# Softmax denominators in two halves, v tiles in halves, and other orders of small work in a graph network kernel

## What is computed

```python
for i in range(NUM_BLOCKS):                       # 4
    y = cond_layer_norm(x, cond, s1_w[i], s1_b[i], b1_w[i], b1_b[i])
    q, k, v = y @ wq[i] + bq[i], y @ wk[i] + bk[i], y @ wv[i] + bv[i]     # 4 heads of 128
    scores = (q[src] * k[dst]).sum(-1) * 128 ** -0.5
    ex = exp(scores - segment_max(scores, src)[src])
    out = segment_sum(ex[..., None] * v[dst], src) / segment_sum(ex, src)
    x = x + out @ wo[i] + bo[i]
    y = cond_layer_norm(x, cond, s2_w[i], s2_b[i], b2_w[i], b2_b[i])
    x = x + relu(y @ m_w1[i] + m_b1[i]) @ m_w2[i] + m_b2[i]
```

## Time and profile before

| quantity | value |
|---|---|
| median of 3 executions | 3040.24 us |
| the profiled execution | 3037.72 us, span of its instructions 3036.0 us |
| PE busy | 2839.1 us |
| DVE busy | 2028.1 us |
| ACT busy | 917.6 us |
| POOL busy | 615.7 us |
| mean granted PE clock | 0.973 of full speed |

### The profile page before, as it was taken

The page is one execution under the profiler, slowest core; times in us unless marked ns, Lnnn a source line. Parts: engine busy times, 40 slices in busy tenths (PEclk is TensorE's granted clock), DMA queues, the critical chain, the costliest instruction groups (busy, mean ns, idle before and its releaser), DMA issues.

```text
span 3036.0 us, 31287 instructions
## 1 busy us (share of the span) xinstructions
PE 2839.1 (94%) x11232; PEld 1806.2 (59%) x11232; DVE 2028.1 (67%) x3758; ACT 917.6 (30%) x1315; POOL 615.7 (20%) x494
## 2 busy tenths in 40 slices
PE   2889989998999999999999999999899999999999
PEld 0346656675556676556666555667545566456555
DVE  8889867786746777757776765778787876623211
ACT  4558732223312223212222221222322213213221
POOL 0000043342113334023334031334310000000000
PEclk9899999999999999999999999999999999999999
DMA  4000020002300000400000320000245244420001
GB/s 108 1 1 1 21 77 1 28 1 66 104 21 1 1 28 15 132 32 14 1 28 15 93 70 14 1 28 1 83 118 152 70 134 137 132 78 37 14 1 34
DMA packets 74966, 143.63 MB, mean 47 GB/s; under 512 B 11684, under 2 KB 12107, under 8 KB 74812
## 3 DMA queue, kind: packets, MB, share of 16 engines
q1 hardware_dynamic: 69276, 129.61, 14.3%
q0 software_dynamic: 5536, 12.03, 1.2%
HBM read 130.68 MB, written 10.92 MB: 47 GB/s over the span
## 4 chain that ended last, share of the span: by engine, by line
PE 73%; DVE 17%; issue 5%; ACT 3%; DMA 1%; DVEq 1%; POOL 0%; POOLq 0%; ACTq 0%
PE ps L1680 14%; PE ps L1903 11%; PE ps L1932 10%; PE ps L1774 6%; PE ps L1877 5%; PE ps L1585 5%; PE ps L1652 4%; DVE prob L1087 4%; DVE x L1077 3%; PE ps L1602 2%; PE ps L1924 2%; PE ps L1763 2%; DVE ps L1030 2%; PE ps L1748 2%; ACT prob L1454 2%
## 5 line engine op out<-in xcount | busy, mean ns | idle before, releaser
L721 POOL TENSOR_TENSOR pacc<-pacc,prob 125x628 f32<-125x628 f32 (+1 forms) x288 | 404.8, 1405 | 349.8 <-DVE prob L1106 349.8
L1680 PE MATMUL ps<-yT,w 128*128 128x416 f32 (+1 forms) x1152 | 439.8, 539 | 15.0 <-DVE qk_lo L1021 5.9
L1774 PE MATMUL ps<-prob,big 125*128 125x314 f32 x1280 | 393.7, 430 | 14.1 <-DVE prob L1106 10.8
L1454 ACT ACTIVATE prob<-prob 125x628 f32<-125x628 f32 x320 | 233.0, 728 | 575.1 <-DVE prob L1087 575.1
L1932 PE MATMUL ps<-pieces,counts_r 125*125 125x512 f32 x1400 | 354.5, 407 | 0.0
L1680 PEld LDWEIGHTS ps<-yT,w 128*128 128x128 f32 x1152 | 227.8, 200 | 201.3 <-issue 187.6
L1106 DVE SCALAR_TENSOR_TENSOR prob<-prob,typed 125x628 f32<-125x628 f32 x320 | 260.2, 813 | 70.2 <-ACT prob L1454 67.6
L1932 PEld LDWEIGHTS ps<-pieces,counts_r 125*125 125x125 f32 x1400 | 258.2, 186 | 77.2 <-issue 17.4
L1763 PE MATMUL ps<-qk_hi 128*125 128x314 f32 x640 | 271.4, 424 | 11.5 <-DVE prob L1087 11.3
L1774 PEld LDWEIGHTS ps<-prob,big 125*128 125x128 f32 x1280 | 227.5, 189 | 81.1 <-DVE prob L1106 27.2
L1030 DVE CUSTOM_DVE_ANT_0 ps<-ps,typed 125x628 f32<-125x628 f32 x320 | 257.8, 816 | 8.0 <-PE ps L1748 7.5
(11 more groups left out here) (222 smaller groups left out, 4282.6 us busy)
## 6 DMA issues: line engine op xcount, KB each, us to landing
basis<-in_basis SPq DMA_DIRECT2D x160, 256.0 KB, 2.7
lite_ring<-in_basis SPq DMA_DIRECT2D x120, 256.0 KB, 2.6
w<-in_m_w SPq DMA_DIRECT2D x8, 1024.0 KB, 6.8
w<-in_wk SPq DMA_DIRECT2D x5, 1024.0 KB, 6.3
w<-in_wv SPq DMA_DIRECT2D x4, 1024.0 KB, 5.6
oT<-in_cw SPq DMA_DIRECT2D x8, 512.0 KB, 3.9
w<-in_wq SPq DMA_DIRECT2D x4, 1024.0 KB, 5.6
w<-in_wo SPq DMA_DIRECT2D x4, 1024.0 KB, 5.5
```

The source lines that it names most:

```text
L721: nc.gpsimd.tensor_tensor(pacc[:, c0:c0 + nn], pacc[:, c0:c0 + nn], prob[:, n % 3, p0:p0 + nn], ALU.add).then_inc(psum_done, 1)
L1454: A.activation(prob[:, n % 3, :], prob[:, n % 3, :], ACT.Exp, scale=DH ** -0.5).then_inc(exp_done, 1)
L1680: last = mm(lin_ps(job, 128, nn), weight[:, k, m * 128:(m + 1) * 128], lhs[:, k, c0:c0 + nn], start=(k == 0), stop=(k == KD - 1))
L1774: last = mm(o_halves[:, b, :], vrow[:, t, h * DH:(h + 1) * DH], prob[:, n % 3, b * QUARTER:(b + 1) * QUARTER], start=(t == 0), stop=(t == ...
```

## The change

1. `row_product` takes the pieces it shall do. In the edge loop a v tile's first two pieces are multiplied at the norm step, the other two four edge steps later.
2. The count copies go to seven places (`TURNED`): three in `prob`, two in `pacc`, two in `shift`. ACT's first `max_row` waits for all masks and for the DMAs out of `shift`, POOL's first sum for those out of `pacc`.
3. In block 0 the second matrices are copied by ACT before the first projection and their low rows made by DVE after its low parts. In later blocks POOL waits for the last `xn` of the norm before it stacks, too.
4. `norm_tiles` does what stands beside the last tile after its last `tile_scale`.
5. The maxima are not negated; the identity by which `max_row` multiplies is.
6. Denominators are made in two halves: tiles 0 to 4 at step 13 (DVE reads them at step 14), tiles 5 to 9 between the second and the third projection of head h+2. Before, all stood behind `max_row`.

Renamed semaphores and tiles are left out of the diff:

```diff
+TURNED = 7
+DEN_AT, DEN_TILES = T + 3, (range(0, T // 2), range(T // 2, T))
+PARTS = {None: range(6), 0: range(0, 1), 1: range(1, 4), 2: range(4, 6), 3: range(2, 6), 4: range(1, 2), 5: range(2, 4)}
...
+        early = w.take()
         project(h + 2, 0)
-        project(h + 2, 1)
+        project(h + 2, 4)
+        g["den"][h] = (early, w.take())
+        project(h + 2, 5)
         max_row(h + 1)
-        g["den"][h] = w.take()
         project(h + 2, 2)
...
+            b = s % TURNED
+            if b < 3:
+                return prob[:].rearrange("p s n -> p (s n)").bitcast(F16)[:, b * N:(b + 1) * N]
+            home = pacc if b < 5 else shift
+            return home[:].bitcast(F16)[:, ((b - 3) % 2) * N:((b - 3) % 2 + 1) * N]
...
-                    if half == 0:
-                        if i == 0:
-                            pool.wait_ge(mneg_ready, 1)
+                    if half == 0 and i:
+                        pool.wait_ge(xn_ready, at(i, 2 * T, T))
                         stack_matrices(1, at(i, 32, 32))
                         nc.gpsimd.drain().then_inc(cw_ready, 1)
...
+                            if i == 0 and n == 0:
+                                for b in (3, 4):
+                                    pool.wait_ge(crow_out[b], 16 * len(range(b, T, TURNED)))
...
-            def matrices_low(signal, count):
-                dve.wait_ge(signal, count)
+            def matrices_low(ln, count):
+                dve.wait_ge(cw_hi, count)
+                mine = cw[:, 2 * ln:2 * ln + 2, :]
                 for rows in (slice(32, 64), slice(96, 128)):
-                    V.tensor_tensor(cw[rows, 0:2, :], stage[rows], cw[rows, 0:2, :].bitcast(F32), ALU.subtract)
+                    V.tensor_tensor(mine[rows], stage[rows], mine[rows].bitcast(F32), ALU.subtract)
...
-                    if t < T and beside is not None:
+                    if t < T - 1 and beside is not None:
                         beside(t)
+                if beside is not None:
+                    beside(T - 1)
...
-                def negate_max(h):
+                def join_max(h):
                     V.drain()
-                    V.tensor_tensor(mx[:], mxp[:, :, 0], mxp[:, :, 1], ALU.max)
-                    V.drain()
-                    V.tensor_scalar(nmx[:], mx[:], -1.0, None, ALU.mult)
-                    V.drain().then_inc(neg_max_ready, 1)
+                    V.tensor_tensor(mxr[:], mxp[:, :, 0], mxp[:, :, 1], ALU.max)
+                    V.drain().then_inc(max_ready, 1)
...
+                if i == 0:
+                    matrices_low(1, 2)
...
+                def reciprocals(h, half):
+                    job, t0, t1 = g["den"][h][half], DEN_TILES[half][0], DEN_TILES[half][-1] + 1
+                    dve.wait_ge(lin_full, job.full)
+                    V.tensor_scalar(rden[:, t0:t1], lin_ps(job, P, t1 - t0, t0), 1.0e-30, None, ALU.max).then_inc(lin_empty[job.slot], 1)
+                    V.drain()
+                    V.reciprocal(rden[:, t0:t1], rden[:, t0:t1])
+                    return V.drain()
...
+                        if j == DEN_AT + 1:
+                            reciprocals(h, 0)
                     if h + 1 < HEADS:
-                        negate_max(h + 1)
+                        join_max(h + 1)
                     if h + 2 < HEADS:
                         low_parts(h + 2, 0)
-                        low_parts(h + 2, 1)
-
-                    job = g["den"][h]
-                    dve.wait_ge(lin_full, job.full)
-                    V.tensor_scalar(rden[:], lin_ps(job, P, T), 1.0e-30, None, ALU.max).then_inc(lin_empty[job.slot], 1)
-                    V.drain()
-                    V.reciprocal(rden[:], rden[:])
-                    V.drain().then_inc(sums_read, 1)
+                        low_parts(h + 2, 4)
+                    reciprocals(h, 1).then_inc(sums_read, 1)
                     if h + 2 < HEADS:
+                        low_parts(h + 2, 5)
                         low_parts(h + 2, 2)
...
-                    matrices_low(cw_hi, i + 2)
+                    matrices_low(0, i + 3)
...
-                if s >= 3:
-                    act.wait_ge(crow_out[s % 3], 16 * (s // 3))
-                    act.wait_ge(mneg_ready, s - 2)
+                if s >= TURNED:
+                    act.wait_ge(crow_out[s % TURNED], 16 * (s // TURNED))
+                    act.wait_ge(mneg_ready, s - TURNED + 1)
...
+                    act.wait_ge(stage_in, 32)
+                    A.activation(cw[:, 2:4, :], stage, ACT.Copy).then_inc(cw_hi, 1)
...
-            def row_product(job, lhs, t, weight):
-
-                reuse(job)
-                for k in range(KD):
+            def row_product(job, lhs, t, weight, parts=range(KD)):
+
+                if 0 in parts:
+                    reuse(job)
+                for k in parts:
                     last = mm(lin_ps(job, P, D), lhs[:, k, t * P:(t + 1) * P], weight[:, k, :],
                               start=(k == 0), stop=(k == KD - 1))
-                last.then_inc(lin_full, 1)
+                if KD - 1 in parts:
+                    last.then_inc(lin_full, 1)
...
-                    row_product(first["v"][t], yT, t, w[0])
+                    row_product(first["v"][t], yT, t, w[0], range(0, 2))
...
+                if rest == NORM_EVERY // 2 and 4 <= n < T + 4:
+                    row_product(first["v"][n - 4], yT, n - 4, w[0], range(2, KD))
...
+                def denominators(h, half):
+                    job = g["den"][h][half]
+                    reuse(job)
+                    pe.wait_ge(psum_done, at(i, EXPS, h * 2 * T + (half + 1) * T))
+                    for t in DEN_TILES[half]:
+                        last = mm(lin_ps(job, P, 1, t), pacc[:, t * P:(t + 1) * P], ones_f[0:P, 0:1], start=True, stop=True)
+                    last.then_inc(lin_full, 1)
...
+                        if j == DEN_AT:
+                            denominators(h, 0)
                     weighted_values(h, 2 * T - 2)
                     if h + 2 < HEADS:
                         project(h + 2, 0)
                     weighted_values(h, 2 * T - 1)
                     if h + 2 < HEADS:
-                        project(h + 2, 1)
+                        project(h + 2, 4)
+                    denominators(h, 1)
+                    if h + 2 < HEADS:
+                        project(h + 2, 5)
                     if h + 1 < HEADS:
                         max_row(h + 1)
-
-                    job = g["den"][h]
-                    reuse(job)
-                    pe.wait_ge(psum_done, at(i, EXPS, (h + 1) * 2 * T))
-                    for t in range(T):
-                        last = mm(lin_ps(job, P, 1, t), pacc[:, t * P:(t + 1) * P], ones_f[0:P, 0:1], start=True, stop=True)
-                    last.then_inc(lin_full, 1)
                     if h + 2 < HEADS:
                         project(h + 2, 2)
```

More of the change, by code:

```diff
@@ L279, in build @@
         mneg_ready = sem("mneg_ready")
-        crow_out = [sem(f"crow_out{s}") for s in range(3)]
+        crow_out = [sem(f"crow_out{s}") for s in range(TURNED)]
         pre_in = sem("pre_in")
@@ L424, in build @@
         mxp = sl("mxp", [P, T, 2], F32)
[L425 to L427 removed]
+        mxr = sl("mxr", [P, T], F32R)
+        minus_ident = sl("minus_ident", [P, P + 1], F32R)
         rden = sl("rden", [P, T], F32)
@@ L1091, in _ @@
                     for b in range(3):
-                        dve.wait_ge(crow_out[b], 16 * len(range(b, T, 3)))
+                        dve.wait_ge(crow_out[b], 16 * len(range(b, T, TURNED)))
                 for h in range(HEADS):
@@ L1418, in max_row @@
                 def max_row(h):
+                    if i == 0 and h == 0:
+                        act.wait_ge(mneg_ready, T)
+                        for b in (5, 6):
+                            act.wait_ge(crow_out[b], 16 * len(range(b, T, TURNED)))
                     for n, job in enumerate(g["mrow"][h]):
```

21 lines of the change are left out of this document (8 added, 13 removed).

## The result

The changed kernel takes 3032.74 us (median of 12 runs, 3028.55 to 3036.73), the kernel before, run beside it on the same chip, 3040.30 (12 runs, 3038.74 to 3046.32). The ratio is 0.9969, 95% interval 0.9961 to 0.9978: 9.4 us faster (6.7 to 11.9), where 3.4 us slower was forecast. The profiled execution has a span of 3030.6 us, 5.4 shorter than before.

A forecast was written before the change was run, and what follows sets the result against it. PE, busy for 94% of the span, was taken to bound the kernel. Terms -8.9 - 5.2 - 11 + 28.5 = +3.4 gave 3043.6, say 3044 us, range for 8 in 10 3003 to 3057.

The forecast's parts named there:

- (a): Edge loop: v tiles in halves cover the refilling of the rings, a turn 7.0 us instead of 7.85; 8.9 us less.
- (b): Count copies in block 0: seven homes end ACT's wait for a DRAM write; 5.2 us less, bounds 3 and 6.5.
- (c): Heads: denominators in halves shorten the head ends; 18 us less, taken as 11 less, bounds +3 and -18.
- I let the clock fall at half of these ends: Head ends, within (c): clock still falls at 8 of 16 ends, 1.5 us each; 7 us of gain taken back.
- (d): End of the second norm, three times: DVE's mixing behind the norm delays PE's projections; 9.5 us each, 28.5 more.
- operation 4: End of the second norm: DVE's last mixing operation, to stand behind POOL's addition to x for 11.0 + 0.55 us.
- slow restart: End of the second norm: PE's projections after a pause of 15 us take 0.8 us more by the clock.
- operation 4 goes before the long addition: Faster rival, second norm's end: DVE's last mixing operation precedes POOL's addition; (d) becomes -6, total 3009 us; chance 0.27.
- head 3's four ends: End of head 3 in each block, within (c): half of 3.52 us goes, 1.75 less each.
- the clock still falls: Slower rival, ends of heads 0 to 2: projections stay slow; (c) becomes +3, total 3058 us; chance 0.13.
- A turn becomes 0.96 x 2 + 3.43 + 1.64: Edge loop, within (a): two edge groups, the v product and the norm matmuls make a turn of 7.0 us.
- DVE does the low rows first: Count copies, within (b): DVE makes the low rows, 2 x 1.22 = 2.4 us, before its second mask.

The follow-up runs named there:

- e1: The changed kernel with part (d) undone: 3004.75 us, ratio 0.9879 to the kernel before.
- e7: The kernel before with part (c) alone, the denominators in halves: 3027.30 us, ratio 0.9950.
- e5: The kernel before with part (a) alone, the v tiles in halves: 3028.51 us, ratio 0.9960.
- e2: The changed kernel, with POOL's long addition to x made to wait for the four mixing operations: 2998.87 us, ratio 0.9857.
- e4: The changed kernel with POOL's addition to x written as ten operations of one tile each: 3001.79 us, ratio 0.987.
- e8: The kernel before with part (d) alone, the tail of the second norm: 3074.84 us, ratio 1.0108.
- e9: The kernel of e3 with all ten denominators in one job between projections, none amid a head: 3003.74 us, ratio 0.987.
- e12: The kernel of e3 with DVE's low rows of block 0 moved behind the join of head 0's maxima: 2984.19 us, ratio 0.9808.
- e3: The kernel of e2 with POOL's stacking also waiting for the mixing: 2984.77 us, ratio 0.9812 to the kernel before.
- e11: The kernel of e3 run again unchanged: 2985.38 us, ratio 0.9813.

## Why the prediction was wrong

By its own steps; us are against the kernel before, from stamps of the profiled executions.

| part | forecast | found | step |
|---|---|---|---|
| (a) | -8.9 | -13.3 | size of the edge products |
| (b) | -5.2 | -6.5 | size, at the bound given |
| (c) | -11 | -17 | "I let the clock fall at half of these ends" |
| (d) | +28.5 | +29.4 | held |

(The account of the profile: -19.8 up to the first head, -14.5 within the four blocks' heads, +26.9 at the three boundaries, +2.0 from the last head to the end, -5.4 in all. The +26.9 are (d)'s +29.4, from e1's boundaries, and -2.5 that I give to (c). That last share is rough: against the kernel before, the three boundaries are together 1.3 shorter in e7, which has (c) alone, and 1.1 longer in e5, which hasn't got it. The +2.0 at the end is no effect of a part: the stretch is 890.5 to 893.0 us long in all experiments, whichever parts they have, and 890.0 before.)

**(d) held, in mechanism and size.** The forecast had operation 4 asked for 0.13 us behind the addition and a duration of 11.0 + 0.55; it came 0.17 behind and took 11.44. The slow restart priced at 0.8 is 0.7 in the mean of the three (14.25, 13.07 and 14.21 us for 32 instructions, 13.12 each before). The restart was forecast 8.7 later and came 8.6 later (827.19, with the stamps ahead of it 23.8 earlier than in the earlier trace rows). e2 and e4 show the cause as such, by removing the addition and by cutting it up. The rival "operation 4 goes before the long addition" (0.27) didn't occur at any of the three boundaries, nor in e8. e2 makes it occur by a wait and takes 34 us off the changed kernel; the rival's -6 in place of the +28.5 is 34.5.

**(c) is the mis-sized term.** The ends came as worked out: in the mean of four blocks -3.45, -2.65 and -2.05 after heads 0, 1 and 2, against -3.7, -2.0 and -2.2; the halves amid heads cost 1.30 three times and 0.60 once, against 1.5 and 0.55. The raw sum was -18 and the measured one is -17, but that is partly luck: without what comes after head 3 the forecast had -11.4 and the blocks show -14.5, and for head 3's four ends it had -7.0 where the three boundaries show -2.5. What failed is what was laid on the raw sum: "I let the clock fall at half of these ends at 1.5 us each", 7 us. Here it fell at one of the eight ends of heads 0 and 1, 1.7 us, and partly at two of the four of head 2, 0.5 and 0.35. There was no row for the half, it was a middle between two stories; and the 7 doesn't come out of its own words either, since of the 12 us for eight ends the two after head 3 are 3, which leaves 9. In nine profiled kernels with halves the slow end after head 0 is seen in 14 of 36 places, block 0's in every one of the nine, and never in 36 after head 1. What sets block 0 apart isn't settled. The rival "the clock still falls" (0.13) didn't come true: of the eight ends one was slow here, three at most in any kernel with halves. As e9 shows it was the right fear for the wrong arrangement: with twenty narrow instructions together it comes true after head 0. Its price was off too: the +3 leaves out head 3, for which the forecast's own terms give -1.2 a block, so that (c) would have been -2 and the total some 12 us slower instead of 17.

Behind head 3 the forecast had -1.75 a block, and e1's boundaries are 0.8 shorter than the kernel before's. Why so little comes of it stays open.

**(a)'s mechanism was right, its size wasn't.** "A turn becomes 0.96 x 2 + 3.43 + 1.64" took the busy durations of merged edge products, which overlap the product behind them, as the time until the next start. By starts the two groups are 0.81 and 0.63, and the turn 6.61 instead of 7.0. The sentence that followed, "DVE's own work is 6.6", has the measured number, but not shown to be for its reason: DVE is busy for 6.37 of the turn and PE for all of it. That is 0.4 us in each of nine turns, 3.4, and 0.9 behind the last turn.

**(b)** gained 8.5 us in the copies and gave back 2.0 ahead of them, 6.5 in all against 5.2 forecast. The 2.4 us of low rows had been counted, "DVE does the low rows first", inside the copies; they stood ahead of the first mask and showed there with 2.05 (e12). Moving them away brings the first head no earlier, so the two figures aren't independent gains and losses.

**Two readings of rows** were off without moving the sum much. The Trainium skill's rule on two SBUF inputs was said to agree with the earlier trace rows, but the operations of the earlier trace rows read one SBUF tensor and a scalar column: they show that DVE waits, not that two inputs are the condition. And the 2.48 us for twenty denominator instructions "at full clock" were taken at a clock of 0.92; blocks 1 and 2 have 2.34.

So the sign was wrong because three gains were sized 11.7 us too small together, and the loss only 0.9: 3.4 - 11.7 + 0.9 + 2.0 for the end is the profile's -5.4, and the ratio's -9.4 has its interval and the profiled execution of before, 2.5 below the median, between. In the sum each caution (the clock, the longer duration, the bound of 5.2) leant to the same side.

## What to carry to other kernels

Before moving an operation of one engine next to one of another, look up what both read. In these traces a DVE operation with two SBUF inputs, issued behind a POOL addition of 11 us, waited for the whole of it, though it stood on the critical path and POOL didn't, and the cures were cheap: a semaphore wait on the engine that has time (34 us for one line), or the long operation cut into short ones (30 us). A change that shows 0.3% may be a gain of 1.2% and a loss of 0.9%; the idle time in front of one group, 64.0 us instead of 15.0, told this at once, and undoing part by part found a kernel 1.9% faster. And where a term of a sum hangs on the clock, put two cases beside each other with a chance each; a half taken from nowhere was the largest error. Stamps of single executions are compared only from a common start and at the same clock: e12's first mask is 0.9 us earlier when read against e3, and 2.05 when read against e11, which is the same kernel.

## What the runs showed of the hardware

- DVE and POOL took turns by operation: with ten POOL operations of 1.3 us queued, DVE's operation waited for one (1.75 us instead of 0.74) and went in before the second, and POOL's second then took 1.71 us instead of 1.27, at all three boundaries (e4).
- Besides operations with two SBUF inputs, DVE's `TENSOR_SCALAR` with one SBUF tensor stood behind POOL in the kernel before: 9.60 us instead of 0.48 beside an addition of 9.94, and 2.60 instead of 0.49 for the second mask beside the stacking. A low part with one PSUM and one SBUF tensor did not: 0.65 us under an addition of 11.02 (e3).
- Behind ten products of one column in a row (twenty instructions, 2.24 us) the next sixteen projection instructions took 7.54 us in five of the eight ends of heads 0 and 1 and 5.85 in three (e9); behind five in a row (ten instructions, 1.15 us) 5.87 in all eight (changed kernel).
- After a wait of 16 us PE ran its 32 projection instructions in 12.94 to 14.25 us (three boundaries each of the changed kernel and of e8). After a wait of 1.96 us it ran them in 12.97 to 14.40 (e1, e3), in e11 in 11.43 at two boundaries and 13.12 at the third. The length of the wait alone doesn't tell what the restart costs.
